# A CIN tower on one Trainium2 core: gathers of the first tile placed earlier and later in GpSimd's program

## The reference

```python
e = jnp.stack([tbl_0[ids[:, 0]], ..., tbl_31[ids[:, 31]]], axis=1)      # 1024 x 32 x 16
for W in (W0, W1, W2):                                                   # each to 64 maps
    xk = jax.nn.relu(jnp.einsum('bmd,bhd,mhk->bkd', x0, xk, W))          # x0 = e
    outs.append(jnp.sum(xk, axis=2))
z = jnp.concatenate(outs, axis=1)
h = jnp.concatenate([z, dense_ctx], axis=1)
h = jnp.maximum(h @ W_top1 + b_top1, 0.0)
h = jnp.maximum(h @ W_top2 + b_top2, 0.0)
y = h @ W_top3
```

## Time and profile before

| | |
|---|---|
| median of 3 runs | 620.2 us (619.76 to 620.31) |
| profiled execution | 619.78 us, of which the span is 618.0 |
| PE busy | 562.0 us, 91% of the span |
| DVE busy | 554.5 us, 90% |
| POOL busy | 468.6 us, 76% |
| ACT busy | 299.5 us, 48% |
| DMA | 246 GB/s in the mean |

### The profile page before, as it was taken

The page is one execution under the profiler, slowest core; times in us unless marked ns, Lnnn a source line. Parts: engine busy times, 40 slices in busy tenths (PEclk is TensorE's granted clock), DMA queues, the critical chain, the costliest instruction groups (busy, mean ns, idle before and its releaser), DMA issues.

```text
span 618.0 us, 8180 instructions
## 1 busy us (share of the span) xinstructions
PE 562.0 (91%) x2752; PEld 206.1 (33%) x2752; DVE 554.5 (90%) x281; ACT 299.5 (48%) x1366; POOL 468.6 (76%) x354
## 2 busy tenths in 40 slices
PE   0058889999999999999999999899998999999997
PEld 0012222334333443334333433234332433334334
DVE  0067899999999999999999999989998999999991
ACT  0021607574357535674366535674346544774331
POOL 6748888888888888888888888888888885125450
PEclk9998999999999999999999999999999999999999
DMA  6297979792699819893699719793498809892000
GB/s 171 79 382 254 394 250 396 241 397 82 209 359 330 294 51 374 297 399 108 218 351 339 299 40 379 265 400 130 171 397 309 329 3 319 316 406 100 1 2 0
DMA packets 54252, 152.02 MB, mean 246 GB/s; under 512 B 9697, under 2 KB 18913, under 8 KB 54210
## 3 DMA queue, kind: packets, MB, share of 16 engines
q1 hardware_dynamic: 46018, 149.39, 64.7%
q0 software_dynamic: 8192, 2.11, 2.6%
HBM read 147.26 MB, written 4.20 MB: 245 GB/s over the span
## 4 chain that ended last, share of the span: by engine, by line
PE 48%; POOL 23%; DVE 10%; issue 9%; DMA 6%; SPq 1%; ACT 1%; DVEq 0%; POOLq 0%
PE acc L570 43%; POOL emb L323 14%; DVE zd L406 10%; POOL zg L335 9%; DMA rolled<-x_scratch 5%; PE mlp L613 2%; SPq L287 1%; PE mlp L604 1%; PE mlp L605 1%; PE acc L579 1%; PE mlp L620 0%; DVE zpart L382 0%; PE mlp L586 0%; ACT xk_sb L472 0%; DMA emb<-tables_in,index 0%
## 5 line engine op out<-in xcount | busy, mean ns | idle before, releaser
L406 DVE TENSOR_TENSOR zd<-rolled,xk_ps 128x2048 f32<-128x2048 f32 x239 | 530.0, 2279 | 16.2 <-PE acc L570 9.2
L570 PE MATMUL acc<-zd,w_sb 128*64 128x512 f32 x1672 | 384.6, 597 | 8.4 <-DVE zd L406 8.4
L323 POOL DMA_INDIRECT emb<-tables_in,index x256 | 244.6, 955 | 75.3 <-issue 64.3
L335 POOL TENSOR_TENSOR zg<-rolled,xk_sb 128x1024 f32<-128x1024 f32 x94 | 223.8, 2382 | 52.0 <-ACT xk_sb L472 18.9
L570 PEld LDWEIGHTS acc<-zd,w_sb 128*64 128x64 f32 x1672 | 119.7, 138 | 242.5 <-issue 210.4
L472 ACT ACTIVATE xk_sb<-acc 64x512 f32<-64x512 f32 x128 | 75.7, 591 | 64.4 <-PE acc L570 61.9
L570 PE MATMUL acc<-zg,w_sb 128*64 128x512 f32 x376 | 98.6, 601 | 6.9 <-POOL zg L335 6.9
L570 PE MATMUL acc<-zd,w 128*64 128x512 f32 x256 | 61.6, 601 | 37.4 <-DVE zd L406 37.4
L472 ACT ACTIVATE xk_ps<-acc 64x512 f32<-64x512 f32 x126 | 71.8, 570 | 30.1 <-PE acc L570 27.2
L451 ACT ACTIVATE relu_ab<-acc 128x16 f32<-128x16 f32 x480 | 78.9, 294 | 8.3 <-PE acc L570 8.3
L451 ACT ACTIVATION_READ_ACCUMULATOR relu_ab<-acc 128x1 f32 x480 | 79.3, 322 | 0.0
(11 more groups left out here) (45 smaller groups left out, 101.0 us busy)
## 6 DMA issues: line engine op xcount, KB each, us to landing
rolled<-x_scratch SPq DMA_DIRECT2D x256, 512.0 KB, 9.4
base<-x_scratch SPq DMA_DIRECT2D x16, 512.0 KB
emb<-tables_in,index POOLq DMA_INDIRECT x256
x_scratch<-emb SPq DMA_DIRECT2D x32, 128.0 KB
w_sb<-w_in SPq DMA_DIRECT2D x2, 512.0 KB, 4.9
wt<-wtop_in SPq DMA_DIRECT2D x1, 512.0 KB, 6.3
wt1a<-wtop_in SPq DMA_DIRECT2D x1, 256.0 KB, 5.5
w<-w0a_in SPq DMA_DIRECT2D x1, 160.0 KB, 2.3
```

Of the source, the lines that this page charges most:

```text
L323: pool.indirect_dma_start(emb[:, i % 2, c * DIM:(c + 1) * DIM], None, tables, bass.IndirectOffsetOnAxis(index[:, g:g + 1].bitcast(U32), 0) ...
L335: nc.gpsimd.tensor_tensor(zg[:, n % ZG_BUFS, :], rolled[:, s, j, :], xk_sb[:, s, :], ALU.mult).then_inc(zg_ready, 1)
L406: nc.vector.tensor_tensor(zd[:, n % ZD_BUFS, 0:w, :], rolled[:, s, j:j + w, :], repeated(layer_in, w), ALU.mult).then_inc(zd_ready, 1)
L570: end = nc.tensor.matmul(acc[h * MAPS:(h + 1) * MAPS, bank, :], weights, z[:, h * HALF:(h + 1) * HALF], start=(j + c == 0), stop=(i == len ...
```

## The change

The number of gathers ahead of the pause goes from 24 to 28, and of those right behind it from 8 to 4. Behind the products of (0,1,0) stand 3 and 0 gathers instead of 4 and 7; behind that of (0,2,0) 7 instead of 3; behind those of (1,1,0) 4 and 5 instead of 3 and 4; behind that of (0,2,1) 8 instead of 7. Of the stretch's 28 gathers 27 are left there, so all later ones stand one place on. DVE's four one-channel products of (0,0,0) lie two to a buffer, in the first two of the three buffers, instead of one to a buffer with the fourth again in the first.

```diff
-GATHERS_FIRST = 24
-GATHERS_EARLY = 8
+GATHERS_FIRST = 28
+GATHERS_EARLY = 4
...
-GATHERS_AFTER_AT = {(0, 1, 0): [4, 7], (0, 2, 0): [3], (1, 1, 0): [3, 4], (0, 2, 1): [7],
+GATHERS_AFTER_AT = {(0, 1, 0): [3, 0], (0, 2, 0): [7], (1, 1, 0): [4, 5], (0, 2, 1): [8],
...
+        def zd_of(q, n, w):
+
+            return zd[:, n // 2, n % 2:n % 2 + 1, :] if q == 0 else zd[:, n % ZD_BUFS, 0:w, :]
...
-                    if n >= ZD_BUFS:
+                    if q > 0:
...
-                    nc.vector.tensor_tensor(zd[:, n % ZD_BUFS, 0:w, :], rolled[:, s, j:j + w, :],
+                    nc.vector.tensor_tensor(zd_of(q, n, w), rolled[:, s, j:j + w, :],
...
-                        z = zd[:, n % ZD_BUFS, c, :] if who == "dve" else zg[:, n % ZG_BUFS, :]
+                        z = zd_of(q, n, w)[:, c, :] if who == "dve" else zg[:, n % ZG_BUFS, :]
```

## The result

The changed kernel takes 626.35 us in the median of 5 runs (624.12 to 626.91), the kernel before 619.76 (619.32 to 620.31): a ratio of 1.0099, interval 1.0082 to 1.0117. The profiled execution took 625.73 us for a span of 623.9, 5.95 us more than before's 619.78. The forecast was 4.35 more.

The account below looks back on a forecast made before the run. POOL's unbroken chain of products and gathers was taken to bound the kernel's middle and fix its end. Entering it 4.35 us late gave 619.78 + 4.35 = 624.1, plus 0.4 for the median: 624.5; range 622.7 to 626.6.

Parts of the forecast that it names:

- The mechanism: POOL from product 4 on: one unbroken chain; any later entry arrives whole at 472.30 and the end; 4.35 us late.
- the base load of stream 1: SP, first tile: issue put at 54.9, not before about 54.6 nor after the 55.62 of the kernel before.
- PE's and DVE's lateness there: At stream 3's first product: DVE and PE 3.8 us late, not added to POOL's 4.35; the later one decides.
- the 0.6 by which product 3 comes later: POOL, first tile: product 3 at 74.3 instead of 73.69, from product 2 at 63.2 plus 11.03.
- in any case: DVE, stream 0's layer 1: its products end at 58.29 with or without the change.
- The step by which the evacuation begins at 60.75: ACT, stream 0's layer 1: square of stream 1's base ends at 60.7, so evacuation begins at 60.75, not 60.2.
- the likeliest case: POOL enters its chain 4.35 us late, 624.5; bounds 623.6 to 625.3; chance 0.70.
- the case that stream 3 stops POOL: POOL's product 12 waits for stream 3; 1 to 2 us on top, 625.5 to 626.5; chance 0.14.
- Blocking of DVE by gathers: DVE's first products held by the four gathers: 0.5 to 3.8 us added, 625.0 to 628.3; chance 0.07.
- The rule that the prediction weighed: A two-SBUF-input DVE instruction and a GpSimd one reading SBUF block each other; put at nothing, 628.3 with full blocking.
- Faster: Earlier layer 1 and base load pass through, slack swallows POOL's lateness: 619.5 or up to 4 us less; chance 0.04.
- no change: POOL's lateness met by about as much slack: 620.2 +- 1; chance 0.05.

Follow-up runs that it names:

- The table alone: The kernel before with only the new table of gathers behind single products, 24/8 split and old buffers kept: 628.34 us, ratio 1.0116.
- the buffers: The kernel before with only the change of DVE's first buffers: 620.46 us, ratio 1.0008.
- the one with extra matmuls: The kernel before with 11 matmuls that add nothing to the output ahead of the first layer: 621.98 us, ratio 1.002.
- the table of before: The changed kernel with the gathers behind single products put back as before, 28/4 split and new buffers kept: 625.33 us, 1.0073 of before.
- the second profile of the same kernel: The changed kernel run again, unchanged, on another chip: 633.54 us, ratio 1.0209; its profiled execution took 632.48 us.
- the split alone: The kernel before with 28 gathers ahead of the pause and 4 behind it, nothing else: 625.98 us, ratio 1.0076.

## Why the prediction was right in sign and 1.6 us short

**The mechanism was right.** Lateness at the entry of POOL's chain arrives whole: 5.26 us at product 6, 5.14 at product 69, and PE's waits for POOL remain. The gathers that were moved behind product 2 cost what they were put at: product 3 to product 6 took 24.35 us before and 28.12 now, 3.77 more, where three gathers at 1.25 make 3.75. The table alone does it, the buffers do nothing. On SP the base load of stream 1 was put at 54.9 and came at 54.33, ahead even of the earliest time allowed for it (54.6, counted from 52.7, where the rows have the DMA engines nearly full to 52.5); stream 2's store at 87.7 and came at 88.55, stream 3's store at 117.3 and came at 117.52, and DVE's first product of stream 3 at 128.4 and came at 128.03; PE's and DVE's lateness there lay beneath POOL's, as forecast.

**The term that was mis-sized is the 0.6 by which product 3 comes later: it measured 1.49.** (Its own terms, 63.2 + 11.03, make 74.2, which is 0.5.) The prediction let product 2 start at 63.2, and had the layer's last DVE products end at 58.29 "in any case". They ended at 55.15 + 4.48 = 59.63, because DVE began layer 1 at 43.56 and not at 42.23. Of these 1.33 us, 0.42 came in with the first rolled load, and 0.9 from PE's longer matmuls. PE's 1.94 behind them makes 61.57, and ACT began at 61.66, released by PE. The step by which the evacuation begins at 60.75, held by the square of the base, failed: the square ended at 60.03 and held nothing. Its upper bound for that step, 61.41, was near by accident, since it came from another engine. What was missed is the kind of dependence. The times of the first layer were those of one execution. In the kernels with 24 or 26 gathers first, DVE's first product of layer 1 lay between 41.84 and 43.50, apart from the one with extra matmuls, and with the table of before it made no difference, because gathers stood between products 1 and 2: with 42.66 product 6 stood at 98.77, with 42.91 at 97.39. With the gathers gone, product 2 follows the start of DVE one to one, as the two profiles of the changed kernel show.

**The tail had no term.** From product 69 (+5.14) to the end (+5.95) the 0.80 us are one wait, that of DVE for a rolled load at 552.97, which before's profile hasn't: DVE's products are 5.1 us late ahead of it and 5.94 from there to the last. SP issued those 16 loads from 541.00, 4.87 us later than before, and took 13.10 us for them instead of 12.04. In the second profile of the same kernel, where everything is over 12 us late, they take 11.09 and DVE doesn't wait, so this term belongs to the execution and not to the change. So 4.35, 0.79 more at product 69 (5.14 less 4.35) and 0.80 make 5.94, what was measured.

**The range held by luck.** The sum, 624.5, is 1.85 us below the median. The bounds set for the likeliest case, 623.6 to 625.3, don't hold the measured 626.35 (and take the lower one from the profiled execution and the upper one from the median). The range's top of 626.6 was there for the case that stream 3 stops POOL, which this kernel's profile doesn't show; a longer first layer and a wait in the tail, neither with a term in the sum, filled the room made for it.

**The rivals.** Blocking of DVE by gathers fell: with gathers all through them DVE's four products take 2.42 (for two), 1.23 and 1.23 us and end at 39.02, where they ended at 38.75. It is some of POOL's gathers that stretch: to 1.46 and 1.03 us in the changed kernel, to 1.69 and 1.39 in its second run, in place of 0.94; the one at 36.14, beside a product of DVE as well, keeps its 0.94. The rule that the prediction weighed (the Trainium skill, "SBUF — State Buffer", section "Who interferes with whom") is borne out in so far as the two seem to meet, with the waiting on POOL's side, between nothing and 0.75 us of it. Stream 3 stopping POOL happened with the table alone, at 1.56 us, which is part of its 628.34. Faster and no change never came near: product 2 didn't start before 58.9.

**What stays open** is the stall of the first layer, 7 us, on two of the chips used, in each of the five kernels with 28 gathers ahead of the pause, and in none with 24. The traces show what is late (the release of ACT and DVE by PE, and SP's issues) and with which edit it comes. It isn't confined to the first layer, as the second evacuation of the split alone shows. Why is not settled. The traces of those two chips, of kernels without the stall as well, hold only 6,100 to 6,600 semaphore updates where those of the other chips hold over 10,500, so part of what would show it isn't recorded, and that difference itself may belong to it. What is recorded points at the updates: from 41 to 48 us the five stalled kernels hold 10 to 12 of them, one each 0.7 us, where the kernels with 24 gathers on the same two chips hold 54 to 63 and the changed kernel's first profile 174. The semaphore that PE updates at the end of the first layer (40.73 in the kernel before, 42.06 in the changed one) has its updates at 48.84 and 48.90 in the second run. So the update comes late, and not the engines' answer to it; whether the gathers hold it up, or the recording does, no run here tells. Nor was a kernel with 28 gathers run a second time on a chip whose traces are full, or one with 26 on the others. The forecast's range, 622.7 to 626.6, holds the time measured first, and not the 633.54 of the changed kernel there.

## What to carry to other kernels

Before you move work out from under a wait, look at what the next wait hangs on. Here the seven gathers in front of product 2 were free, since product 3 had to wait for another engine anyway; taken from there, they left 10 us of idle time on the engine that paces the kernel, and came back as a delay that nothing absorbed. An engine that never pauses for 400 us, and is waited for at the end of them, passes on each microsecond by which it enters that stretch late, so its idle time ahead of it is to be filled and not made. And a hand-written order in which an engine arrives a little late may be hiding the spread of others between executions and chips: the same change cost 1.0% on one chip and 2.1% on another.

## What the runs showed of the hardware

Gathers issued by POOL while DMA loads fill the engines and DVE multiplies can go with a semaphore release that comes 8 us late (40.85 to 48.92), and with DMA issues on SP at 18.82 us for 16 in place of 11.46. Here it did so on two chips and not in the changed kernel's first profile.

The same stretch of matmuls doesn't run at the same speed in each profile. From PE's first matmul to the first one that takes less than 1.06 us it was 2.6 us in the profile of before, 4.3 in the changed kernel's first and 5.1 in its second; the 20 matmuls of the first layer took 6.0 us in the first of these and 6.9 in the second.

DVE's 128x1024 products with both inputs in SBUF took 1.21 to 1.23 us with gathers beside them as without; single gathers beside them took up to 1.69 us in place of 0.94.
